# One PSUM bank instead of two for turning the attention probabilities

## The reference

```
x = x + attention(layernorm(x))
x = x + experts(layernorm(x))
attention: 16 heads; q has 128 + 64 columns a head (the last 64 rotated), keys and values
           come from 64 latent columns (layer-normed) and one rotated key of 64
           weights = softmax(q k^T * scale); out = (weights v) Wout
experts:   8 routed experts of width 176 (top 2 of a softmax) and a shared one of width 352
```

## Time and profile before

| | |
|---|---|
| median of three runs | 800.9 us (784.86 to 806.77) |
| the profiled execution | 781.86 us, span 780.1 us |
| TensorE busy | 733.0 us (94% of the span) |
| VectorE busy | 543.7 us (70%) |
| GpSimd busy | 508.9 us (65%) |
| ScalarE busy | 437.5 us (56%) |
| mean granted TensorE clock | 0.990 |

### The profile page before, as it was taken

The page is one execution under the profiler, slowest core; times in us unless marked ns, Lnnn a source line. Parts: engine busy times, 40 slices in busy tenths (PEclk is TensorE's granted clock), DMA queues, the critical chain, the costliest instruction groups (busy, mean ns, idle before and its releaser), DMA issues.

```text
span 780.1 us, 17956 instructions
## 1 busy us (share of the span) xinstructions
PE 733.0 (94%) x5924; PEld 708.6 (91%) x5924; DVE 543.7 (70%) x1269; ACT 437.5 (56%) x1158; POOL 508.9 (65%) x587
## 2 busy tenths in 40 slices
PE   7969999999899999999999998999999998999997
PEld 7759889999899999998899998999999998999997
DVE  6679878597647975498745976379754987369543
ACT  3669754586418842297416863198523974169421
POOL 5438558684768846686566847688465955679244
PEclk9999999999999998999999999999999999999999
DMA  8940000000000000000000000000000000000000
GB/s 239 285 137 2 2 14 1 29 2 3 13 2 27 0 13 0 0 27 0 13 0 27 0 4 10 0 27 0 13 0 7 20 0 13 0 15 1 1 1 14
DMA packets 20226, 18.76 MB, mean 24 GB/s; under 512 B 2816, under 2 KB 19680, under 8 KB 20192
## 3 DMA queue, kind: packets, MB, share of 16 engines
q1 hardware_dynamic: 19360, 18.13, 7.6%
q10 hardware_dynamic: 832, 0.21, 0.1%
HBM read 16.23 MB, written 2.10 MB: 23 GB/s over the span
## 4 chain that ended last, share of the span: by engine, by line
PE 39%; POOL 25%; issue 20%; DVE 7%; ACT 3%; POOLq 1%; DVEq 0%; ACTq 0%
PE ps_q L245 19%; POOL probs L1394 11%; PE ps_y L245 10%; POOL qswap L1384 6%; POOL qf L1389 5%; PE ps_s L245 3%; PE ps_o L245 2%; PE ps_t L1001 1%; PE ps_t L926 1%; ACT qswap L1084 1%; DVE q_lo L305 1%; DVE qf L1212 1%; PE ps_o L887 1%; PE ps_t L1041 1%; DVE score L1270 1%
## 5 line engine op out<-in xcount | busy, mean ns | idle before, releaser
L1394 POOL TENSOR_TENSOR probs<-probs,rinv 128x512 f32<-128x512 f32 x128 | 131.5, 1040 | 56.3 <-DVE rinv L1225 56.3
L1166 ACT ACTIVATE probs<-ps_q 128x256 f32<-128x256 f32 (+1 forms) x112 | 42.9, 383 | 159.3 <-PE ps_q L245 158.6
L400 POOL TENSOR_TENSOR pT_hi<-probs,one 128x256 fp32r<-128x256 f32 x112 | 75.2, 672 | 82.9 <-DVE probs L1320 61.8
L1110 ACT ACTIVATE probs<-ps_s,nmax 128x256 f32<-128x256 f32 x256 | 119.1, 476 | 14.6 <-DVE nmax L1221 13.6
L1317 DVE TENSOR_TENSOR probs<-ps_q,probs 128x256 f32<-128x256 f32 x88 | 37.3, 424 | 102.7 <-ACT probs L1166 96.1
L1389 POOL TENSOR_TENSOR qf<-qf,qswap 128x512 f32<-128x512 f32 x63 | 91.8, 1458 | 17.5 <-DVE qf L1212 9.2
L1084 ACT ACTIVATE qswap<-ps_q 32x512 f32<-32x512 f32 x128 | 75.5, 590 | 44.0 <-PE ps_q L245 42.4
L305 DVE TENSOR_TENSOR pT_lo<-ps_t,pT_hi 128x512 fp32r<-128x512 f32 x128 | 86.8, 678 | 13.5 <-ACT pT_hi L1084 13.4
L1221 DVE TENSOR_REDUCE nmax<-ps_s 128x2 f32<-128x512 f32 x128 | 87.3, 683 | 10.3 <-PE ps_s L245 8.3
L1384 POOL TENSOR_TENSOR qswap<-qswap,qsin 128x512 f32<-128x512 f32 x63 | 81.1, 1287 | 18.5 <-ACT qswap L1084 18.5
L245 PE MATMUL ps_s<-kT_hi,q_hi 128*128 128x256 f32 x256 | 78.8, 308 | 12.4 <-DVE q_lo L305 8.8
(11 more groups left out here) (208 smaller groups left out, 2512.0 us busy)
## 6 DMA issues: line engine op xcount, KB each, us to landing
wq_raw<-Wq_dram SPq DMA_DIRECT2D x16, 192.0 KB, 4.3
xnext<-x_dram SPq DMA_DIRECT2D x8, 256.0 KB, 2.8
wout_raw<-Wout_dram SPq DMA_DIRECT2D x8, 256.0 KB, 4.8
xin<-x_dram SPq DMA_DIRECT2D x8, 256.0 KB, 2.7
out_dram<-x SPq DMA_DIRECT2D x8, 256.0 KB, 2.2
mg_raw<-w_gate_dram SPq DMA_DIRECT2D x4, 352.0 KB, 6.5
mu_raw<-w_up_dram SPq DMA_DIRECT2D x4, 352.0 KB, 6.6
md_raw<-w_down_dram SPq DMA_DIRECT2D x3, 384.0 KB, 6.0
```

What stands on the lines that cost most here:

```text
L400: return gp.tensor_tensor(hi, src, ones.to_broadcast(list(src.shape)), ALU.mult)
L1110: last = nc.scalar.activation(probs[h % 3][:, j, :], L.ps_s[h % 2][:, j, :], ACT.Exp, bias=nmax[:, h, j:j + 1], accum_out=rsum[:, h, j:j + 1])
L1166: nc.scalar.activation(gate[m % 2][0:rows, :], L.ps_q[m % 2][0:rows, 0, :], ACT.Silu).then_inc(ev.silu_done.sem, 1)
L1394: gp.tensor_tensor(probs[h % 3][:, :, :], probs[h % 3][:, :, :], rinv[:, h, :].unsqueeze(2).to_broadcast([P, NT, S]), ALU.mult).then_inc(e ...
```

## The change

Every head is turned into `ps_t[0]`. So that the bank is free, turn(h) now waits for probs_lo(h-1) where it waited for probs_lo(h-2), and turn(1) for probs_lo(0). The copies and the subtractions read `ps_t[0]`. No instruction is added, taken out or moved on any engine; only the wait of `turn` and the bank in three places differ. `ps_t[1]` is unused in attention and is still used by the experts.

```diff
             def turn(i, h):
                 pe.wait_ge(ev.pn_done.sem, ev.pn_done.upto(i, h + 1))
-                if h < 2:
+                if h == 0:
                     pe.wait_ge(ev.cb_done.sem, ev.cb_done.before(i, ER))
                 else:
-                    pe.wait_ge(ev.plo_done.sem, ev.plo_done.upto(i, h - 1))
+                    pe.wait_ge(ev.plo_done.sem, ev.plo_done.upto(i, h))
                 for c in range(NT):
                     for j in range(NT):
-                        last = nc.tensor.transpose(L.ps_t[h % 2][:, c, tile(j)], probs[h % 3][:, j, tile(c)], L.ident[:, :])
+                        last = nc.tensor.transpose(L.ps_t[0][:, c, tile(j)], probs[h % 3][:, j, tile(c)], L.ident[:, :])
                 last.then_inc(ev.t_full.sem, 1)
...
-                copy(pT_hi[h % 3][:, :, :], L.ps_t[h % 2][:, :, :]).then_inc(ev.phi_done.sem, 1)
+                copy(pT_hi[h % 3][:, :, :], L.ps_t[0][:, :, :]).then_inc(ev.phi_done.sem, 1)
...
-                minus_hi(pT_lo[h % 3][:, :, :], L.ps_t[h % 2][:, :, :], pT_hi[h % 3][:, :, :]).then_inc(ev.plo_done.sem, 1)
+                minus_hi(pT_lo[h % 3][:, :, :], L.ps_t[0][:, :, :], pT_hi[h % 3][:, :, :]).then_inc(ev.plo_done.sem, 1)
```

## The result

| | before | after |
|---|---|---|
| median of the runs | 793.63 us (4 runs, 784.86 to 806.77) | 876.15 us (4 runs, 872.92 to 876.72) |
| the profiled execution | 781.86 us | 872.92 us |
| mean granted TensorE clock | 0.990 | 0.954 |

The kernel became slower: the ratio is 1.115, with a 95% interval from 1.108 to 1.123. The prediction was 859 us, with a range of 838 to 886. This ratio holds something that is not the change's. In all four runs of the changed kernel TensorE's clock was low during the set-up (the profile shows it for one, the times say it of the others), which costs some 22 us and happened in only 6 of the 20 runs of the kernel before beside e10.

A forecast was written before the change was run, and what follows sets the result against it. TensorE and VectorE, both nearly full, were taken to bound the kernel; odd turns' waits chain them, 7.7 us in each of eight attentions, 61.6 us. On 781.9 that gives 843.5, plus 15.6 for run level: 859 us, range 838 to 886.

The forecast's parts named there:

- The first rival: TensorE's clock falls in the new holes of attention: one fall in each gives 875 us, two 891; chance 0.18.
- The mechanism: Odd turns wait for VectorE, whose next scores queue behind them: one whole VectorE lap between odd turns, 7.7 us an attention.
- The even turns: Turn(2r) waits for probs_lo(2r-1), bank free after 2.65 us; TensorE's own 2.5 to 3.3 us hides it, so costed at nothing.
- The semaphore: Signal from the end of VectorE's subtraction to the waiting turn, estimated at 0.05 us in the first lateness and each lap.
- The moments: VectorE's moments of the next sequence, 2.02 us in the lap to turn(7), now delaying the turn itself.
- The bare evacuation: Turn, copy, subtraction and semaphores with nothing between, 2.02 us from turn to turn; applied to turn(14) and turn(15) only.
- The end: Turn(14) and turn(15) each wait for a bare evacuation: 4.04 us after turn(13), leaving turn(15) 7.7 us late.
- The level: 15.6 us added because the runs shown lay that far above the profiled execution in the mean: 843.5 became 859 us.
- No cost at all: GpSimd sets the pace through rounds 1 to 5, so TensorE may be late for nothing: 801 us; chance 0.02.
- only the first lateness: VectorE has slack, so laps don't add up and only turn(1)'s 1.94 us is paid: 817 us or less; chance 0.03.
- Query_lo leaves GpSimd's shadow: VectorE's query_lo runs alone, at 0.68 us, instead of beside GpSimd's rotation, up to 1.71: 841 us; chance 0.07.
- The signs that I named: Profile signs: turns idle behind the subtraction, VectorE idle before maxima, TensorE some 87% busy; wrong if clock under 1 inside attention.

The follow-up runs named there:

- e10: The kernel before (two banks), with 56 instead of 40 idle transposes at TensorE's start: median 782.96 us in ten runs.
- e1: The changed kernel's new wait on every turn, but with both banks kept in turns: 850.35 to 873.06 us, ratio 1.086 to the kernel before.
- e2: The kernel before with both banks, the new wait on even turns alone: 782.98 us, ratio 0.999.
- e3: The kernel before with both banks, the new wait on odd turns alone: 856.25 us, ratio 1.092.
- e12: The changed kernel (one bank) with 56 idle transposes and scores(2r+2) ahead of turn(2r-1) on TensorE: 816.88 us, ratio 1.044.
- e11: The kernel before (two banks) with 56 idle transposes and scores(2r+2) ahead of turn(2r-1) on TensorE: 786.24 us, ratio 1.005.
- e13: The changed kernel with 56 idle transposes and VectorE's normalising of the next sequence moved behind probs_lo(13): 850.90 us, ratio 1.087.
- e14: The changed kernel with 56 idle transposes and turn(2r) ahead of attend(2r-2) on TensorE: 850.96 us, ratio 1.087.
- e6: The changed kernel (one bank) with 56 instead of 40 idle transposes at TensorE's start: median 851.48 us, ratio 1.087.
- e4: The changed kernel (one bank) with probs_lo(2r-2) taken first in VectorE's round, ahead of query_lo: 850.56 us, ratio 1.085.

## Why the prediction was right, step by step

**What was luck.** The measured 876.15 us holds 22 us of a set-up at the low clock, which no term and no rival had, and the forecast 859 held 15.6 us for a cause not known. What the working was about is the cost of the wait, 61.6 us forecast and 68.5 measured at the same clock in the set-up; that part was not luck. The first rival's figure, 875 us, is near the measured time by chance too: the falls inside attention cost some 4.5 us and not its 16.

**The mechanism held.** The wait, not the bank, costs (e1); odd turns carry it and even turns next to nothing (e2, e3); and the scores that VectorE needs, queued behind the turn that waits for VectorE, close the loop (e12 against e11). The even turns were costed at nothing and measured at 0.3 us an attention.

**The terms.** All in us, for an attention with the clock up (i = 5 after against i = 3 before):

| term | forecast | measured |
|---|---|---|
| lateness of turn(1), with the one of turn(0) taken off | 1.94 | 2.06 |
| turn(1) to turn(3) | 6.33 | 6.37 |
| turn(3) to turn(5) | 6.01 | 6.24 |
| turn(5) to turn(7), with the moments | 7.55 | 6.82 |
| turn(7) to turn(9) | 5.28 | 5.44 |
| turn(9) to turn(11) | 4.75 | 5.40 |
| turn(11) to turn(13), with the normalising | 5.74 | 5.65 |
| turn(13) to turn(15) | 4.04 | 4.34 |
| an attention in all, over before | 7.7 | 8.4 |

Four terms were mis-sized.

- *The semaphore.* I put 0.05 us between VectorE's end and the turn; it is 0.15 (596.61 to 596.76). That is 0.1 us in the first lateness and in each lap.
- *The moments.* 2.02 us were taken from before, where the last small operation had lasted 1.04 us of them beside GpSimd. After the shift GpSimd stood still there, it lasted 0.17, and the whole took 1.13. The same displacement that I bounded for query_lo I had not asked of the moments.
- *The bare evacuation in laps 5 and 6.* The step "even turns cost nothing" looked at what an even turn waits for, not at what it makes the odd turn behind it wait for. I had that chain (2.02 us from turn to turn) and used it for turns 14 and 15 only. From turn(9) to turn(11) it binds: 5.40 against 4.75 (e13, e14).
- *The end.* Two bare evacuations at 2.02 each: from turn(13) to turn(14) it was 2.21 (with 0.18 of waiting only, the rest is TensorE's own work), from 14 to 15 2.13.

The errors of opposite sign left 0.7 us an attention, 8 x 8.36 = 66.9 us instead of 61.6.

**The first rival came true in part.** The clock fell in six of eight attentions of the profiled execution. But it cost less than I had worked out from the experts. Behind turn(1), four times, the first step was 6.73 instead of 6.37 us: turn(3) had waited for 0.81 us there, and that went first. Behind turn(7), twice, it cost 1.53 us: from turn(7) to turn(8), a stretch without any wait, TensorE took 4.85 instead of 3.29 us. Together some 4.5 us, which with the 66.9 make the 71.1 of the table to 0.3. I had expected the fall at turn(7)'s hole and a hole of 3.1 us; it was 2.22, since the moments were shorter. My reading of the earlier trace rows was wrong besides: I called it a stretch with gaps, but its row has TensorE busy for 11.97 of 12 us, and in the 6 us ahead of it the longest idle time is 0.50 us. So that fall had no hole in front of it, and what set it off is open. And a granted clock under 1 inside attention, which I had named as a sign of being wrong, did occur.

**The level.** I added 15.6 us because the runs shown lay that far above the profiled execution. The cause was not known; it is the clock of the set-up, and an execution has it or doesn't: some 783 or some 804 us before, 851 or 873 after. With the measured terms it comes to 783.0 + 66.9 + 3.0 (the falls in e6's attentions: four behind turn(1), one behind turn(7)) = 852.9 us, against 851.5 measured, or some 20 more with the low set-up; the 859 lay between two levels at which no run was. The six profiles with 40 transposes say that an execution's own start decides: how early the idle transposes go over to the fast pace, and so how long the gap is. The changed kernel's four runs were all at the slower level, and why all four is open: with e1, e3 and e4, whose TensorE starts with the same instructions, it was 4 of 13 runs.

**The other rivals.** "No cost at all" and "only the first lateness" are refuted by the steps. "Query_lo leaves GpSimd's shadow" didn't occur: it took 1.60 and 1.46 us in the first laps, against 1.71 and 1.39. The measurement in the Trainium skill, "TensorE: Matmul & The Clock Gate", section "HAM oscillation — how this bites in real kernels", where double buffering in PSUM brought 126.6 to 125.5 us, doesn't carry over: here the second bank is worth 8.7%. The rule on the other side in the Trainium skill, "Perfetto Trace Analysis", section "Matmuls", is that independent groups should rotate through banks so that the emptying of one overlaps the next. The 8.7% agree with it; e1 adds that it is the freedom from the wait that counts.

**The signs that I named.** TensorE's share fell to 88% (87 foretold), at 32 us more busy time with the same number of instructions. Of these, 19 us go with the low clock in the set-up: e6, without it, is busy for 745.8 us. VectorE's idle time went where it was foretold, in front of the maxima.

No version here beats the kernel before. What the 56 transposes bring is its shorter time in every run (783.0 us).

## What to carry to other kernels

When a change makes a wait earlier, don't ask only how late the awaited event is: look at what is queued behind the waiting instruction, and follow it until it comes back. If it comes back to the engine that is waited for, the cost is a whole lap of both engines each time, and then the order of two instructions may be worth more than the buffer (34.6 us here). And a floor that is not the longest chain in one lap may be in the next: work out each lap against all of them.

## What the runs showed of the hardware

- A short gap at the start can set TensorE's clock for a long stretch. Behind a gap of 2.52 us at 8 us the granted clock was at the lower level, 1.2 GHz, from some 12 to 66.7 us, though TensorE was busy 53.5 of the 56 us from 12 to 68; filling 1.3 us of the gap kept this long fall away in 44 runs of 44.
- Transposes alone brought TensorE from the slow to the fast pace: in e6 it did nothing but idle transposes, 11 of them from 2 to 4 us and 21 from 6 to 8. The granted clock reads 1.00 in both stretches, so at the very start the pace of the instructions tells more than that column. "TensorE: Matmul & The Clock Gate" in the Trainium skill says in "Part 4: PE-mode transpose" that transposes don't count as busy in the same way and don't bring the full clock. The start of e6 differs from that, and the measurement decides. The set-up after the fall, mostly transposes, would fit it.
- A fall of the clock costs what its place leaves: 0.36 us ahead of a wait of 0.81 us, 1.53 us in a stretch of TensorE without one (both in the profile of the changed kernel).
- From one turn over copy and subtraction to the next turn of the same bank: 2.11 us (0.64 to the copy, 0.63 to the subtraction, 0.84 to the turn), in e4.
